# Decay exponents from DRAM rows instead of matmuls, and the rotary additions moved from VectorE to GpSimd

## The chip, the cores and the metric

The kernel runs on one core of a Trainium2 chip. The metric is the device time of one execution in microseconds (us). The kernel before took 1953.01 us, the median of three runs (1952.74 to 1956.06).

## What is computed

A block of a transformer: a routed bias mix, a gated linear attention layer with decay, and the routed bias mix once more, on 2048 tokens of 512 features. Nearly all of the time goes into the attention layer, cut here to what matters (L = 2048, 32 query heads H, 8 key and value heads KVH, head size D = 128, chunks of 128 tokens):

```python
q = (x @ Wq.T).reshape(B, L, H, D);  k, v = ...          # 8 key heads, each repeated for 4 query heads
q, k = q * cos + rot(q) * sin, k * cos + rot(k) * sin    # rot swaps the halves of a head
dt = softplus(x @ Win.T + dt_bias);  g = dt * -exp(A_log_bias)
G = cumsum(g)                                            # inside each chunk, for each head
decay = where(i >= j, exp(G[i] - G[j]), 0)
y_intra = (q @ k.T * decay) @ (v * dt)
state = state * exp(G[-1]) + (k * exp(G[-1] - G)).T @ (v * dt)      # carried from chunk to chunk
y = y_intra + (q * exp(G)) @ state_before
out = (y / rms(y) * gnorm_w * silu(x @ Wg.T)) @ Wo.T
```

## The kernel before

**Tiling.** The outer loop goes over the 8 key heads, called groups g, each with its G = 4 query heads. Inside a group, 16 chunks n of 128 tokens follow each other, since the state is carried. One chunk is one step of every engine. The 4 heads of a group lie side by side in tiles of 128 x 512. Every matmul operand is split into a bf16 high part (suffix H, by ScalarE) and a bf16 low part (suffix L, the remainder), and `mm3` (L286 to L290) issues three matmuls: high by high, high by low, low by high. Matmuls are thus the same three lines everywhere; the operand names tell them apart.

**Fills.** Projections are made one block of 4 chunks (512 tokens) ahead, in ten items: key 0, queries 1 to 4, values 5, gates 6 to 9. `FILLS` puts them in slots A, B and C of the steps: items 0, 1, 2 in step 0 of a block, 3, 4, 5 in step 1, 6, 7 in step 2, and 8, 9 in step 3. Each goes to one of two PSUM banks used in turn (RING, shared with the output projection `project_out`), and a fill waits on `ring_free`, until the bank's last user but one has been read.

**An item's way.** For the key and each query: ScalarE copies the swapped halves (`swap`, QS), VectorE multiplies by the cosines (`rotate` part 0, L1209, which frees the bank), GpSimd multiplies QS by the sines (`times_sin`, L1031), VectorE adds (`rotate` part 1, L1213), ScalarE rounds to bf16 (`hi`, L838 and L840), and the low part is taken: for items 0 and 3 on GpSimd (`lo`, L1036 and L1038), for 1, 2 and 4 on VectorE (`q_lo`, L1217). The turned key is put on B_T by `turn_keys` in step 1 of a block; ScalarE reads it in `keys_hi` (KDH) and VectorE in `keys_lo` (KDL), which frees the bank B_T that the next `turn_z` needs.

**Decay.** GpSimd writes the masked tables MH and ML (`masked_g`, L1049 and L1050) and DM (`masked_dt`, L1054). TensorE multiplies a triangle with MH and ML (L693 and L694), which gives G[i] - G[j] in the bank B_D. ScalarE takes the exponential into PF (L864). VectorE multiplies the scores by DM (L1241) and by PF (L1244). ScalarE and GpSimd split PF into PH and PL (L869, L1077).

**Order.** Every engine runs its own instruction list, written out by hand in its `step`, in order; semaphores link them. The loop over groups is `Fori`; it holds chunks 1 to 15 of one group and chunk 0 of the next. The end of a step on VectorE is `gated` (which waits for GpSimd's RR, L1084), `keys_lo` in step 1 of a block, `add_out`, and then `decayed` of the next step. On ScalarE the end of step 1 is `hi` of item 4 and then `keys_hi`. Weights of the next group are loaded and split in steps 10 to 13 (VectorE L1300, GpSimd L1025), the output weights in step 1 (VectorE L1296). SyncE issues these DMAs, one after the other.

Of the kernel before, what the change touches and what calls it, by code (L numbers as in the profile page):

```python
# [34 lines left out]
EPS = 1e-5  # L35
GW = G * P
# [8 lines left out]
MID = {10: (2,), 11: (5,), 12: (7,), 13: (9,)}  # L45
N_EARLY = sum(len(i) for i in EARLY.values())
# [48 lines left out]
def build(nc, x, cos, sin, masks, wall, rwt, rb, eb2, wint, dtb, alog, gn, out):  # L95
    with ExitStack() as ctx:
# [30 lines left out]
        GH = sb("GH", [P, NCH * H], BF16)  # L127
        GL = sb("GL", [P, NCH * H], BF16)
        IDF = sb("IDF", [P, P])
        MB = sb("MB", [P, 3, P], BF16)  # L130
        DM = sb("DM", [P, G, P])
# [15 lines left out]
        B_S, B_D, B_PV, B_IN, B_CS, B_T = BANK[2:8]  # L147
# [11 lines left out]
        MH = sb("MH", [P, G, P], BF16)  # L159
        ML = sb("ML", [P, G, P], BF16)  # L160
# [18 lines left out]
        with ExitStack() as over:  # L179
# [27 lines left out]
        LTB, TRIB, IDB = MB[:, 0, :], MB[:, 1, :], MB[:, 2, :]  # L207
# [7 lines left out]
        logdecay_full = Sem("logdecay_full", NCH, free=1)  # L215
# [16 lines left out]
        s_ready = Sem("s_ready", NCH, free=1)  # L232
        ql2_ready = Sem("ql2_ready", NB * 3, free=1)
# [8 lines left out]
        ql_ready = Sem("ql_ready", NB * 2, free=2)  # L242
        m_ready = Sem("m_ready", NCH)
        dm_ready = Sem("dm_ready", NCH)
# [22 lines left out]
        d_dot, d_x, d_abs, d_e, d_e2, d_g, d_gh, d_gl, d_cum, d_exp, d_wj = (Sem(n, 1) for n in (  # L267
            "d_dot", "d_x", "d_abs", "d_e", "d_e2", "d_g", "d_gh", "d_gl", "d_cum", "d_exp", "d_wj"))
# [38 lines left out]

        @block.sync
        def _(sp):
# [10 lines left out]
            def load_weights(g):  # L320
                for i in range(NPIECE):

                    if 2 <= i < PO + 2:
                        signal, k = wl_of(i - 2)
                        sp.wait_ge(signal.sem, signal.at(g, k))
                    else:
                        sp.wait_ge(wol_ready.sem, wol_ready.at(g, (i - 2 - PO) if i > PO else i - 2))
                    sp.dma_start(STAGE[:, i % 2, :], wall[g, i] if isinstance(g, int)
                                 else wall[bass.ds(g, 1), i].rearrange("a p n -> (a p) n")).then_inc(w_landed[i % 2].sem, 16)
            load_weights(0)  # L330
            with sp.Fori(1, KVH) as g:
                load_weights(g)
# [290 lines left out]
        def _(pe):  # L623
            for signal in (cs_full, inter_full, intra_full, kt_full, logdecay_full, zt_full):
                pe.sem_inc(signal.sem, signal.free)
# [5 lines left out]
            for k in range(NB):  # L631
# [819 lines left out]
```

## Time and profile before

| | |
|---|---|
| median of three runs | 1953.01 us |
| the profiled execution | 1956.19 us, of which its span is 1954.4 us |
| busy TensorE, matmuls | 1765.2 us (90%) |
| busy VectorE | 1548.2 us (79%) |
| busy GpSimd | 1417.8 us (73%) |
| busy ScalarE | 1032.4 us (53%) |
| mean granted TensorE clock | 0.969 of full speed |
| one group of 16 chunks (809.26 to 1028.90) | 219.64 us |

The profile is taken in one execution and names engines PE (TensorE matmuls), PEld (its weight loads), DVE (VectorE), ACT (ScalarE), POOL (GpSimd). Instructions overlap a little at their ends: a matmul with 512 columns is shown as 379 ns, and the next one starts about 216 ns after it; on POOL and DVE the next instruction starts some 40 and 80 ns before the end shown of the one before. So lengths of a sequence are taken from starts. In a timeline row the bracket gives how long the engine sat idle before, and which instruction ended the wait.

### The profile page before, as it was taken

The page shows a single profiled execution, that of the slowest core. Times are in us where ns is not written, and L with a number is a line of the kernel's source. Part 1 is how long each engine was busy: PE and PEld are TensorE (multiplying, and loading weights), DVE is VectorE, ACT ScalarE, POOL GpSimd, SP SyncE. Part 2 cuts the span into 40 slices and gives each one's busy share as a digit, 9 for nine tenths or more (in the row PEclk, how much of TensorE's full clock was granted, in tenths as well). Part 3 has the DMA queues.
Part 4 walks back from the last instruction along what each step waited for, and adds up shares of the span by engine and source line. Part 5 has one row for each costly group of instructions (what it writes and reads, how often), then busy time and mean ns, then how long its engine had stood idle before and what let it go on. Part 6 is the DMA issues. An engine that isn't in the chain of part 4 may idle for free.

```text
span 1954.4 us, 38786 instructions
## 1 busy us (share of the span) xinstructions
PE 1765.2 (90%) x11904; PEld 997.8 (51%) x11904; DVE 1548.2 (79%) x2955; ACT 1032.4 (53%) x2620; POOL 1417.8 (73%) x1348
## 2 busy tenths in 40 slices
PE   5777998999999998999998998999999998999976
PEld 4544554545455554555454554555455554555544
DVE  6967778787887778787887778787887778787875
ACT  5445555555555555555555555555555555555542
POOL 1348787777777777777777787777777787777743
PEclk9689999999999999999999999999999999999997
DMA  4100001000010001000010001000010001000002
GB/s 162 33 17 23 1 1 49 9 23 2 28 28 24 1 1 49 8 23 2 28 28 24 1 1 49 8 23 2 28 28 24 1 1 46 10 12 1 1 1 86
DMA packets 19515, 43.36 MB, mean 22 GB/s; under 512 B 2656, under 2 KB 3168, under 8 KB 18144
## 3 DMA queue, kind: packets, MB, share of 16 engines
q1 hardware_dynamic: 19296, 40.64, 6.6%
q8 instruction: 113, 1.85, 0.4%
q14 instruction: 106, 0.87, 0.1%
HBM read 36.44 MB, written 4.19 MB: 21 GB/s over the span
## 4 chain that ended last, share of the span: by engine, by line
PE 33%; DVE 22%; issue 18%; POOL 15%; ACT 9%; DVEq 1%; ACTq 0%; POOLq 0%; DMA 0%
PE B L288 10%; PE B L290 9%; PE B L289 9%; DVE YF L1289 2%; POOL QS L1031 2%; POOL WVL L1073 2%; POOL MH L1049 2%; POOL WVF L1065 2%; POOL ML L1050 2%; DVE QF L1209 2%; POOL DM L1054 2%; POOL RR L1084 2%; DVE PF L1244 2%; DVE QF L1213 2%; DVE DM L1241 2%
## 5 line engine op out<-in xcount | busy, mean ns | idle before, releaser
L288 PE MATMUL B<-WH,XTH 128*128 128x512 bf16 (+1 forms) x1024 | 291.6, 306 | 46.6 <-DVE QF L1209 33.5
L1077 POOL TENSOR_TENSOR PL<-PF,PH 128x512 bf16<-128x512 f32 x128 | 155.0, 1211 | 208.3 <-ACT PH L869 208.3
L290 PE MATMUL B<-WH,XTL 128*128 128x512 bf16 (+1 forms) x1024 | 291.2, 305 | 0.0
L289 PE MATMUL B<-WL,XTH 128*128 128x512 bf16 (+1 forms) x1024 | 291.2, 305 | 0.0
L288 PE MATMUL B<-XTH,WH 128*128 128x512 bf16 x640 | 242.7, 379 | 9.8 <-DVE G L1229 7.8
L288 PE MATMUL B<-WH,ZTH 128*128 128x512 bf16 x512 | 194.7, 380 | 53.8 <-DVE QF L1209 33.5
L289 PE MATMUL B<-XTL,WH 128*128 128x512 bf16 x640 | 242.6, 379 | 0.0
L290 PE MATMUL B<-XTH,WL 128*128 128x512 bf16 x640 | 242.6, 379 | 0.0
L869 ACT ACTIVATE PH<-PF 128x512 bf16<-128x512 f32 x128 | 80.8, 631 | 304.6 <-DVE PF L1244 304.6
L1031 POOL TENSOR_TENSOR QS<-QS,SIN 128x512 f32<-128x512 f32 x160 | 228.6, 1429 | 5.2 <-ACT QS L832 5.2
L1305 DVE TENSOR_TENSOR ZTL<-B,ZTH 128x512 bf16<-128x512 f32 x128 | 88.1, 688 | 143.0 <-ACT ZTH L899 143.0
L1049 POOL TENSOR_TENSOR MH<-MB,GH 128x512 bf16<-128x512 bf16 x128 | 133.7, 1045 | 90.3 <-PE B L694 90.2
L290 PE MATMUL B<-WH,ZTL 128*128 128x512 bf16 x512 | 194.0, 379 | 0.0
L289 PE MATMUL B<-WL,ZTH 128*128 128x512 bf16 x512 | 194.0, 379 | 0.0
L892 ACT ACTIVATE SQ<-B 128x128 f32<-128x128 f32 x512 | 134.6, 277 | 80.9 <-DVE B L1256 79.6
L1073 POOL TENSOR_TENSOR WVL<-WVF,WVH 128x512 bf16<-128x512 f32 x120 | 140.2, 1168 | 45.6 <-ACT WVH L876 45.6
L1289 DVE SCALAR_TENSOR_TENSOR YF<-B,RR,G 128x128 f32<-128x128 f32 x512 | 143.6, 342 | 35.0 <-POOL RR L1084 34.9
L288 PEld LDWEIGHTS B<-WH,XTH 128*128 128x128 bf16 x1024 | 103.4, 101 | 128.9 <-DVE QF L1209 39.5
L876 ACT ACTIVATE WVH<-WVF 128x512 bf16<-128x512 f32 x120 | 75.8, 632 | 165.9 <-POOL WVF L1065 165.9
L1084 POOL TENSOR_TENSOR RR<-RM,HALF 128x4 f32<-128x4 f32 x128 | 144.8, 1131 | 19.1 <-POOL RM L1081 16.8
L1278 DVE TENSOR_TENSOR STL<-ST,STH 128x512 bf16<-128x512 f32 x120 | 108.7, 906 | 52.3 <-ACT STH L883 50.2
L1054 POOL TENSOR_TENSOR DM<-MB,DT 128x512 f32<-128x512 bf16 x128 | 143.9, 1124 | 0.0
(164 smaller groups left out, 4984.3 us busy)
## 6 DMA issues: line engine op xcount, KB each, us to landing
STAGE<-in_wall SPq DMA_DIRECT2D x112, 256.0 KB, 2.6
ACC<-in_x SPq DMA_DIRECT2D x4, 1024.0 KB, 7.9
out<-ACC SPq DMA_DIRECT2D x3, 1024.0 KB, 3.9
COS<-in_cos SPq DMA_DIRECT2D x1, 1024.0 KB, 12.9
SIN<-in_sin SPq DMA_DIRECT2D x1, 1024.0 KB, 14.9
out<-ACC SPq DMA_DIRECT2D x4, 256.0 KB, 2.5
EBF<-in_eb SPq DMA_DIRECT2D x1, 256.0 KB, 4.1
MASKS<-in_masks SPq DMA_DIRECT2D x1, 192.0 KB, 4.9
```

Of the source, the lines that this page charges most:

```text
L288: nc.tensor.matmul(out_, ah, bh, start=first, stop=False)
L289: nc.tensor.matmul(out_, ah, bl, start=False, stop=False)
L290: return nc.tensor.matmul(out_, al, bh, start=False, stop=last)
L892: ins = nc.scalar.activation(SQ[:, h, :], B_PV[:, h * P:(h + 1) * P], ACT.Square, scale=float(P) ** -0.5, accum_out=SS[:, h:h + 1])
L1031: nc.gpsimd.tensor_tensor(QS[:, sl, :], QS[:, sl, :], SIN[:, t0:t0 + TB], ALU.mult).then_inc(sin_ready.sem, 1)
L1049: nc.gpsimd.tensor_tensor(MH[:, :, :], tri, tab(GH, g, n)[:, :, None].broadcast_to([P, G, P]), ALU.mult)
L1054: nc.gpsimd.tensor_tensor(DM[:, :, :], TRIB[:, None, :].broadcast_to([P, G, P]), tab(DT, g, n)[:, :, None].broadcast_to([P, G, P]), ALU.mu ...
L1073: nc.gpsimd.tensor_tensor(WVL[:, :], WVF[:, :, :].rearrange("p h e -> p (h e)"), WVH[:, :], ALU.subtract).then_inc(wvl_ready.sem, 1)
L1077: nc.gpsimd.tensor_tensor(PL[:, n % 2, :], PF[:, :], PH[:, n % 2, :], ALU.subtract).then_inc(pl_ready.sem, 1)
L1084: nc.gpsimd.tensor_tensor(RR[:, :], RM[:, :], HALF[:, :], ALU.pow).then_inc(rr_ready.sem, 1)
L1278: nc.vector.tensor_tensor(STL[:, :], ST[:, :], STH[:, :], ALU.subtract).then_inc(stl_ready.sem, 1)
L1289: ins = nc.vector.scalar_tensor_tensor(YF[:, c], B_PV[:, c], RR[:, h:h + 1], G2[:, s + b % 2 * (s == BLK - 1), c], ALU.mult, ALU.mult)
```

## The change

The exponents of the decay no longer come from matmuls. In the preamble the negative cumulative sums (NG) are turned, so that a head's 128 values lie in a row, and are written to DRAM. For every chunk one DMA brings the four heads' rows, broadcast to all 128 partitions, into ROWS (one of two buffers). GpSimd adds a large number where the mask is to be (`mask_rows`), and ScalarE takes exp(-row + NG) in four instructions, one for each head, with the bias by partition. VectorE multiplies scores, dt and decay in four instructions, where it had two of 128 x 512. MH, ML, DM, B_D and their matmuls are gone. Beside this, GpSimd adds the sine part to all five rotated items (`add_sin`) and takes all their low parts (`lo`); VectorE keeps the cosines. GpSimd's and SyncE's steps are written in a new order; ScalarE's and VectorE's keep theirs without the removed instructions.

```diff
+            def load_rows(g, n):
+                at = g + n // NCH
+                if n >= 2:
+                    sp.wait_ge(decay_ready.sem, decay_ready.at(g, n - 2))
+                sp.dma_start(ROWS[:, n % 2, :], (rows_dram[n % NCH, at] if isinstance(at, int)
+                             else rows_dram[n % NCH, bass.ds(at, 1)].rearrange("a n -> (a n)")).partition_broadcast(P)
+                             ).then_inc(rows_landed[n % 2].sem, 16)
...
 def scores(g, n):
-                pe.wait_ge(s_ready.sem, s_ready.at(g, n - 1))
+                pe.wait_ge(p_ready.sem, p_ready.at(g, n - 1))
                 mm3(B_S[:, :], KH[:, par, t:t + P], KL[:, par, t:t + P], QH[:, par, :, t:t + P], QL[:, par, :, t:t + P],
                         True, True).then_inc(scores_full.sem, 1)
-                pe.wait_ge(m_ready.sem, m_ready.at(g, n))
-                pe.wait_ge(decay_ready.sem, decay_ready.at(g, n - 1))
-                nc.tensor.matmul(B_D[:, :], LTB, MH[:, :, :], start=True, stop=False)
-                nc.tensor.matmul(B_D[:, :], LTB, ML[:, :, :], start=False, stop=True).then_inc(logdecay_full.sem, 1)
...
 def decay(g, n):
-                nc.scalar.activation(PF[:, :], B_D[:, :], ACT.Exp).then_inc(decay_ready.sem, 1)
+                for h in range(G):
+                    c = slice(h * P, (h + 1) * P)
+                    ins = nc.scalar.activation(PF[:, c], ROWS[:, n % 2, c], ACT.Exp, bias=tab(NG, g, n)[:, h:h + 1], scale=-1.0)
...
+            def add_sin(g, b, j, use):
+                dst = QF[:, (j - 1) % 2, :] if j else KF[:, :]
+                pool.wait_ge(ring_free.sem, ring_free.at(g, use))
+                pool.wait_ge(sin_ready.sem, sin_ready.at(g, 5 * b + j))
+                nc.gpsimd.tensor_tensor(dst, dst, QS[:, (j + 1) % 2, :], ALU.add).then_inc(qf_ready.sem, 1)
+            def mask_rows(g, n):
+                pool.wait_ge(rows_landed[n % 2].sem, g * (NCH // 2 * 16) + (n // 2 + 1) * 16)
+                rows = ROWS[:, n % 2, :].rearrange("p (h i) -> p h i", h=G)
+                nc.gpsimd.tensor_tensor(rows, rows, AFTER[:, None, :].broadcast_to([P, G, P]), ALU.add).then_inc(rows_masked.sem, 1)
...
 def decayed(g, n):
-                nc.vector.tensor_tensor(dm, B_S[:, :], dm, ALU.mult).then_inc(s_ready.sem, 1)
-                nc.vector.tensor_tensor(PF[:, :], dm, PF[:, :], ALU.mult).then_inc(p_ready.sem, 1)
+                for h in range(G):
+                    c = slice(h * P, (h + 1) * P)
+                    ins = nc.vector.scalar_tensor_tensor(PF[:, c], B_S[:, c], dt[:, h:h + 1], PF[:, c], ALU.mult, ALU.mult)
```

GpSimd, the second half of step 1 of a block, in the kernel before: QS are the sine products of items 3 and 4, RM and RR the norm, then the masked tables of the next step.

```order
L1031 TENSOR_TENSOR QS<-QS,SIN 128x512
L1072 REGISTER_ALU
L1073 TENSOR_TENSOR WVL<-WVF,WVH 128x512
L1054 ISA
L1054 TENSOR_TENSOR DM<-MB,DT 128x512
L1029 REGISTER_ALU
L1031 TENSOR_TENSOR QS<-QS,SIN 128x512
L1081 TENSOR_TENSOR RM<-SS,EPSC 128x4
L1083 REGISTER_ALU
L1084 TENSOR_TENSOR RR<-RM,HALF 128x4
L1049 ISA
L1049 TENSOR_TENSOR MH<-MB,GH 128x512
```

The same place now, from WVL on (the addition to QF is that of item 4, the last query; ROWS is the mask of the next step):

```order
L1113 TENSOR_TENSOR WVL<-WVF,WVH 128x512
L1076 TENSOR_TENSOR QS<-QS,SIN 128x512
L1121 TENSOR_TENSOR RM<-SS,EPSC 128x4
L1123 REGISTER_ALU
L1124 TENSOR_TENSOR RR<-RM,HALF 128x4
L1085 REGISTER_ALU
L1087 TENSOR_TENSOR QL<-QF,QH 128x512
L1080 REGISTER_ALU
L1082 TENSOR_TENSOR QF<-QF,QS 128x512
L1093 REGISTER_ALU
L1095 TENSOR_TENSOR ROWS<-ROWS,AFTER 128x512
```

The addition of item 4 is now GpSimd's, and stands behind the norm and the low part of item 3. VectorE, the end of step 1 before:

```order
L1278 TENSOR_TENSOR STL<-ST,STH 128x512
L1223 TENSOR_TENSOR VL<-B,VH 128x512
L1211 REGISTER_ALU
L1213 TENSOR_TENSOR QF<-QF,QS 128x512
L1289 SCALAR_TENSOR_TENSOR YF<-B,RR,G 128x128 x4
L1234 TENSOR_TENSOR KDL<-B,KDH 128x512
L1309 TENSOR_TENSOR ACC<-ACC,B 128x512
L1241 TENSOR_TENSOR DM<-B,DM 128x512
L1244 TENSOR_TENSOR PF<-DM,PF 128x512
```

And now, up to the low part of the turned key (the addition to QF is gone from between VL and YF):

```order
L1244 REGISTER_ALU
L1249 TENSOR_TENSOR QF<-B,COS 128x512
L1309 TENSOR_TENSOR STL<-ST,STH 128x512
L1254 TENSOR_TENSOR VL<-B,VH 128x512
L1320 SCALAR_TENSOR_TENSOR YF<-B,RR,G 128x128 x4
L1265 TENSOR_TENSOR KDL<-B,KDH 128x512
```

## Rows read from the trace of the kernel before

**Rows 1.** The page: busy time of the engines, busy tenths of PE in 40 slices.

```profile
PE 1765.2 (90%) x11904; PEld 997.8 (51%) x11904; DVE 1548.2 (79%) x2955; ACT 1032.4 (53%) x2620; POOL 1417.8 (73%) x1348
...
PE   5777998999999998999998998999999998999976
```

**Rows 2.** Windows: the four blocks of one group; us, PE, PEld, DVE, ACT, POOL, clock.

```profile
809.26:865.13 55.87, 52.15 (x342) 29.19 (x341) 43.97 (x78) 30.63 (x78) 41.85 (x40) 0.97 0.07 21
865.13:918.13 53.00, 51.52 (x353) 28.30 (x352) 41.26 (x80) 28.04 (x75) 42.21 (x40) 1.00 0.01 1
918.13:973.70 55.57, 51.87 (x353) 28.15 (x352) 45.75 (x83) 29.89 (x79) 43.93 (x40) 1.00 0.08 25
973.70:1028.90 55.20, 50.88 (x350) 27.95 (x349) 45.52 (x78) 30.66 (x79) 43.02 (x42) 1.00 0.09 25
```

**Rows 3.** Timeline of PE in the second block: start, duration, instruction, idle before.

```profile
865.13 0.38 PE L288 MATMUL B<-QH,KH 128*128 128x512 bf16 x1
...
865.77 0.38 PE L693 MATMUL B<-MH,MB 128*128 128x512 bf16 x1
...
866.21 0.38 PE L288 MATMUL B<-XTH,WH 128*128 128x512 bf16 x1
...
899.21 0.61 PE L735 MATMUL B<-IDF,YF 128*128 128x128 f32 x4
...
907.92 0.39 PE L288 MATMUL B<-WH,XTH 128*128 128x512 bf16 x1 [0.53 <-DVE G L1229]
```

**Rows 4.** Instructions of a tile on POOL: shortest, median and longest duration in ns.

```profile
L1031 POOL TENSOR_TENSOR QS<-QS,SIN x160: 1261/1271/1811, 118.7 to 1823.8; 128x512 f32<-128x512 f32 x160
L1077 POOL TENSOR_TENSOR PL<-PF,PH x128: 1152/1158/1600, 148.0 to 1872.6; 128x512 bf16<-128x512 f32 x128
L1065 POOL TENSOR_TENSOR WVF<-VF,WJ x120: 1033/1042/1492, 150.1 to 1864.4; 128x512 f32<-128x512 f32 x120
L1049 POOL TENSOR_TENSOR MH<-MB,GH x128: 1032/1041/1486, 135.3 to 1860.0; 128x512 bf16<-128x512 bf16 x128
L1081 POOL TENSOR_TENSOR RM<-SS,EPSC x128: 192/203/667, 163.0 to 1881.4; 128x4 f32<-128x4 f32 x128
L1084 POOL TENSOR_TENSOR RR<-RM,HALF x128: 1007/1008/1552, 163.3 to 1881.6; 128x4 f32<-128x4 f32 x128
```

**Rows 5.** Timeline of ACT in the second block, swap of item 1 and end of step 1.

```profile
874.02 0.59 ACT L831 ACTIVATE QS<-B 64x512 f32<-64x512 f32 x1 [1.04 <-PE B L290]
...
895.13 0.63 ACT L838 ACTIVATE QH<-QF 128x512 bf16<-128x512 f32 x1 [1.35 <-DVE QF L1213]
895.67 0.58 ACT L858 ACTIVATE KDH<-B 128x512 bf16<-128x512 f32 x1
```

**Rows 6.** Timeline of DVE in the second block, from the last addition on.

```profile
894.42 0.68 DVE L1213 TENSOR_TENSOR QF<-QF,QS 128x512 f32<-128x512 f32 x1
...
897.04 0.68 DVE L1234 TENSOR_TENSOR KDL<-B,KDH 128x512 bf16<-128x512 f32 x1
...
898.24 0.69 DVE L1241 TENSOR_TENSOR DM<-B,DM 128x512 f32<-128x512 f32 x1
898.96 0.69 DVE L1244 TENSOR_TENSOR PF<-DM,PF 128x512 f32<-128x512 f32 x1
...
902.01 0.68 DVE L1229 SCALAR_TENSOR_TENSOR G<-TH,B 128x512 f32<-128x512 f32 x1
...
904.02 1.11 DVE L1270 SCALAR_TENSOR_TENSOR ST<-ST,DCH,B 128x128 f32<-128x128 f32 x4
...
907.19 0.67 DVE L1229 SCALAR_TENSOR_TENSOR G<-TH,B 128x512 f32<-128x512 f32 x1
```

**Rows 7.** Timeline rows around the loop's turn and the weights.

```profile
967.10 2.68 DVE L1300 TENSOR_TENSOR WL<-STAGE,WH 128x512 bf16<-128x512 f32 x2 [1.30 <-ACT WH L816]
...
1046.75 0.60 ACT L864 ACTIVATE PF<-B 128x512 f32<-128x512 f32 x1 [2.93 <-issue]
```

**Rows 8.** The page: DMA issues, KB each, us to landing.

```profile
STAGE<-in_wall SPq DMA_DIRECT2D x112, 256.0 KB, 2.6
```

More of the change, by code:

```diff
@@ new lines, in _, with step @@
+            for f in range(NB):
+                sp.wait_ge(d_rows.sem, d_rows.at(f, 0))
+                sp.dma_start(rows_dram[f * BLK:(f + 1) * BLK].rearrange("c g (h t) -> (c g h) t", h=G), NGT[:, f, :]).then_inc(d_sent.sem, 16)
+                if f == 0:
+                    sp.wait_ge(d_sent.sem, 16)
+                    for n in range(2):
+                        load_rows(0, n)
+            sp.wait_ge(d_sent.sem, 16 * NB)
+            load_rows(0, 2)
+            load_rows(0, 3)
+            def step(g, n, last):
+                if not (last and n >= NCH - 3):
+                    load_rows(g, n + 3)
+                if n == 1:
+                    for i in range(PO + 2, NPIECE):
+                        load_piece(g, i)
+                if not last:
+                    for i in LOADS.get(n, ()):
+                        load_piece(g + 1, i)
@@ L334, in _ @@
+            with sp.Fori(0, KVH - 1) as g:
+                for n in steps(False):
+                    step(g, n, False)
+            for n in steps(True):
+                step(KVH - 1, n, True)
             for k in range(NB - 1):
@@ L1109, in _, with step @@
-            masked_dt(0, 0)
-            masked_g(0, 1)
+            pool.wait_ge(after_ready.sem, 1)
+            mask_rows(0, 0)
+            mask_rows(0, 1)
             p_lo(0, 0)
-            masked_dt(0, 1)
             weighted_v(0, 0)
             wv_lo(0, 0)
-            def step(g, n, last):
+            def step(g, n, last, first=False):
                 b, s = divmod(n, BLK)
-                def sine(x):
-                    if filled(n, last).get(x, PV_) < PV_:
-                        times_sin(g, b + 1, filled(n, last)[x])
+                ring = ring_order(last)
+                now = {x: i for x, i in filled(n, last).items() if i < PV_}
+                before = {x: i for x, i in filled(n - 1, last).items() if i < PV_} if n else {}
@@ L1122, in step, with add @@
                 nxt = not (last and n == NCH - 1)
+                def add(x):
+                    if x in now:
+                        add_sin(g, b + 1, now[x], now[x] - FIRST if first else ring[("F", b, now[x])])
                 if not (last and n >= NCH - 2):
-                    masked_g(g, n + 2)
+                    mask_rows(g, n + 2)
+                if "C" in before:
+                    add_sin(g, (n - 1) // BLK + 1, before["C"], -1 if n == 1 else ring[("F", (n - 1) // BLK, before["C"])])
@@ L1132, in step @@
                 if not filled(n, last):
                     inv_rms(g, n)
[L1134 removed]
+                add("A")
+                if nxt:
                     wv_lo(g, n + 1)
[L1136 to L1140 removed]
+                if "B" in now:
+                    times_sin(g, b + 1, now["B"])
                 if filled(n, last):
```

211 lines of the change are left out of this document (89 added, 122 removed).

## The prediction, made before the changed kernel was run

> **What bounds the kernel now.** I read the page first. TensorE is busy 90% of the span, and nine tenths or more in nearly every slice from the fifth to the last but two; VectorE has 79%, GpSimd 73% [rows 1]. So a matmul that goes should count, unless something else has little slack. The windows by block say how little: the four blocks of a group take 55.87, 53.00, 55.57 and 55.20 us, and GpSimd is busy 42 to 44 us of each [rows 2]. Then the timeline of PE in the second block, the one without weights and without the loop's turn. Its matmuls of 512 columns start 0.216 us apart (three score matmuls take from 865.13 to 865.77) and the pair on MH and ML takes 865.77 to 866.21, 0.43 us [rows 3]. The turn of the gated output in step 2 (L735) starts at 899.21, 34.08 us after the block's start, and the block ends at 918.13, 18.92 later [rows 2, 3]. Between, PE waits once more, 0.53 us (0.70 by starts) for a gate on VectorE [rows 3]. TensorE is the bound, but in every block it meets VectorE's order two or three times.
>
> **What is removed on PE.** 128 pairs of 0.43 us, 55 us in all. This is the most that the change can give, and 1953 less 55 is 1898.
>
> **What moves to GpSimd.** Removed in each step: MH, ML and DM, at about 1.04 us a piece (MH's row; a spacing of 1.00), 12 us a block. Added in each step: the mask on ROWS. No row shows it. It reads two full f32 tiles as the sine product does (1.27) and broadcasts as WVF does (1.04) [rows 4]; I take 1.23, the spacing of the first, which it is nearest to, and keep 1.00. Added in each block: five additions of the sine's form (1.23) and three low parts of PL's form (1.12) [rows 4]: 9.5 us. With the masks, 14.4 us come for 12.0 that go. The sum of GpSimd grows by 2.4 us a block, still under TensorE's. But the masks went from all four steps, and the additions come into the first two.
>
> **The path in steps 0 and 1.** Count from the block's start, T. Fill B of step 0 (item 1) now ends 0.43 earlier than before, so its swap starts at 874.02 less 865.13 less 0.43, or 8.46, takes two halves of 0.6 [rows 5], and GpSimd can begin the sine product at 9.7. From there it has, without a gap that I can find (each input is ready before its turn): sine of item 1, RM and RR, low 0, add 1, sine 2; next step: mask, add 2, PL, low 1, WVF, low 2, sine 3, add 3, WVL, sine 4, RM and RR, low 3, add 4. These are nine of 1.23, six of 1.12, one of 1.00 and two norm pairs (0.20, a gap, 1.01: 1.33 together) [rows 4]: 11.1 + 6.7 + 1.0 + 2.7 = 21.5. Add 4 ends at 31.2 without any lengthening. Durations on GpSimd have a second value 0.44 to 0.54 above the first [rows 4]; I count it once for each STL, the instruction of VectorE left in each step that reads two SBUF tiles while GpSimd is busy: 0.9. So 32.1.
>
> Who waits for add 4? ScalarE, in order: `hi` of item 4, and behind it `keys_hi`, whose input is long there. Before, `hi` waited 1.35 us for VectorE's addition, which started at 894.42, 29.3 after T [rows 5, 6]. From the addition's end it takes `hi` 0.54, KDH 0.58, KDL 0.68 and three handovers, 1.95 us, until B_T is free [rows 5, 6]: 34.05. The turn in step 2 of PE needs B_T. Without waits it would arrive at about 31.2: 34.08 less three pairs of 0.43, less the 1.6 that are left when the matmuls before it are counted at their spacing of 0.216 (a quarter of it for 128 columns, 0.44 for four turns). So it waits some 2.8 us in all, and starts at 34.05: where it started before. **All of PE's gain in steps 0 to 2 is spent there.**
>
> Behind KDL on VectorE stand the output's addition and `decayed`, and for them wait PH, the gate's tanh, ZTH, ZTL and the gate G (902.01). From KDL's end (897.72) to G's (902.69) it took 4.97 [rows 6]. `decayed` was 1.41 (898.24 to 899.65) and is four of ST's form, 1.11 [rows 6], so 4.67. PE needs G 4.35 after its turn (0.44 + 1.32 + 2.59), and waits 0.3. From G to the next G there were 5.18 us [rows 6]; here collisions can take off some 0.3, PE wants it after 3.24 of matmuls, and waits 1.2 to 1.6 where it waited 0.70. The 18.92 held one pair and this wait: 18.92 - 0.43 - 0.70 + 0.3 + 1.3 = 19.4. **Second block: 34.05 + 19.4 = 53.4, against 53.00: 0.4 longer.**
>
> **The other blocks.** Third block, steps 2 and 3: two weight splits on VectorE in each step (2.6 us [rows 7]) make VectorE's loop longer than PE's work. It starts 1.46 later (34.05 against KDL's end at 32.59) and gives back 0.3 a step by the shorter `decayed`: +0.8. Fourth block: GpSimd's split in step 12 is put ahead of the sine of item 2 (1.12), two splits on VectorE lengthen GpSimd by 0.45 each, and the block starts with the wait that the third hands on. Turn at 37.5, and 19.4 less 0.65 (the last chunk updates no state): 56.3 against 55.20, +1.1. First block: the loop's turn costs ScalarE 2.93 us [rows 7] inside the GpSimd path, since `hi` of item 1 now ends late and the exponentials and PH stand behind it: GpSimd waits some 1.2 for PH, and output weights on VectorE lengthen it by 1.4 to 1.8. Turn at 37.5, block 56.9 against 55.87: +1.0.
>
> **Costs put at nothing.** The rows' DMA: a transfer of 256 KB lands in 2.6 us [rows 8], is issued when a buffer is free, at the start of a step, and is used a step later; SyncE queues it behind weight loads only in steps 1 and 10 to 13, where it still has half a step. If a broadcast took three times 2.6 it would be as well. The four exponentials (at most 1.2 against 0.6) stand where ScalarE waited. The preamble adds four turns and four DMAs, and GpSimd's additions there replace VectorE's; it loses four casts: between -3 and +3, taken as 0.
>
> **Sum.** Eight groups of (1.0 + 0.4 + 0.8) and seven fourth blocks of 1.1 (the last group fills nothing there): 17.6 + 7.7 = 25.3. The last four chunks are a loop over VectorE and lose 0.3 each: -1.2. Total +24 us. Against the profiled execution (span 1954.4, 1956.19 in all) that is 1980; the median of the runs lies 3.2 below, so **1977 us, 1.2% slower**.
>
> A rule on the collisions: by the Trainium skill (GPSIMD Engine Reference, Specifications) GpSimd's SBUF interfaces are shared with VectorE and contend with instructions of VectorE that have two SBUF inputs. That speaks for the change here, as the additions leave VectorE; the two values in [rows 4] agree. By this rule two collisions are left in the path, which is what I count; if they cost nothing, the sum would be 0.9 x 31 = 28 us lower, at about 1949.
>
> **Rivals.**
> (A) *GpSimd's path is shorter, and TensorE stays the bound.* For it: the sum of GpSimd grows only by 2.4 us a block, and the mask may cost 1.00. Against it: the list above has no gap, and the path would have to be 3 us shorter in 22. Then steps 0 to 2 save three pairs and steps with gates little: 1.3 us a block, 31 blocks, 40 us: 1913. Half of it, 1935, if the path is 1.5 shorter.
> (B) *Both cancel.* Path at 31.2 + 0.5, so that a block is 0.8 shorter than I say: -0.4 to 0 against before: 1950 to 1957.
> (C) *The longer waits also cost clock.* The first window's clock is 0.97 against 1.00 in the others [rows 2], a loss of 0.03 x 55.87 or 1.7 us at the lower of two levels, after waits of that block. Waits of 3 to 6 us in two blocks of a group could add 16 such stretches, 27 us: 2004. Against it: they would fall where PE waits for gates anyway.
> (D) *Rows come late:* the mask waits for the DMA, in every step by the time beyond the half step. It decides only from a landing of about 8 us on, three times the row; then 1 us a step, 128 steps, 2105. I give it little.
>
> **Chances.** Forecast (1962 to 1995) 0.52; A 0.22; B 0.11; C 0.12; D 0.03. By 0.2% (about what a measurement of this kernel tells from no change): faster 0.25, same 0.10, slower 0.65. The forecast alone reaches 1962 to 1995; the range for 8 in 10 takes in B, half of A, and C: 1930 to 2004.
>
> **What would show it.** In the changed profile: GpSimd without a wait from the sine of item 1 to the addition of item 4, over some 22 us; KDH right behind `hi`, with ScalarE's wait ending on a GpSimd addition at L1082; PE's longest waits before the turn (L735's successor) in step 2 of every block, some 2 to 3 us, ended by VectorE's KDL; GpSimd busy about 1500 us, TensorE's matmul sum less by its 256 instructions, and a mean of PE under 90%. A second block of 53.4, a fourth of 56.3. The prediction is wrong if that wait is under 1 us, or ends on ZTL or a gate instead, if the mask takes under 1.0, or if GpSimd stands idle between those two instructions.

## The result

The changed kernel takes 2014.7 us, the median of four runs (2013.5 to 2020.67); the kernel before, timed beside it, took 1954.53. The ratio is 1.0306, with a 95% interval of 1.0271 to 1.0341: **3.1% slower**. The prediction said slower and gave 1977 with a range that ended at 2004. The direction was right, the size was not: 60 us, not 24. Of the executions of the experiments below one stands apart: one of e11_mask2 took 3567 us, which no profile shows; its interval leaves it out, and without it the median is 2040.6.

### The profile page after: what moved, and what is told of

It reads as the page before. It is cut to its first block, busy times and chain, and to the rows that moved or that the text cites. A ratio compares the mean times of both kernels' runs of the same rounds, so it can differ in the third digit from the quotient of the medians.

```text
span 2018.9 us, 39366 instructions
## 1 busy us (share of the span) xinstructions
PE 1740.0 (86%) x11652; PEld 972.2 (48%) x11652; DVE 1269.7 (63%) x2956; ACT 1117.0 (55%) x3012; POOL 1427.6 (71%) x1340
## 4 chain that ended last, share of the span: by engine, by line
POOL 44%; issue 26%; PE 11%; DVE 10%; ACT 6%; POOLq 1%; DVEq 0%; ACTq 0%; DMA 0%; SPq 0%
POOL QS L1076 10%; POOL QF L1082 7%; POOL QL L1087 6%; POOL WVL L1113 5%; POOL RR L1124 3%; POOL ROWS L1095 3%; POOL WVF L1105 3%; PE B L287 3%; PE B L288 3%; PE B L289 3%; POOL KF L1082 2%; ACT SQ L934 2%; POOL WL L1070 2%; POOL RM L1121 1%; DVE PF L1274 1%
## 5 line engine op out<-in xcount | busy, mean ns | idle before, releaser
L1117 POOL TENSOR_TENSOR PL<-PF,PH 128x512 bf16<-128x512 f32 x128 | 150.9, 1179 | 276.9 <-ACT PH L911 276.5
L1076 POOL TENSOR_TENSOR QS<-QS,SIN 128x512 f32<-128x512 f32 x160 | 210.5, 1315 | 12.3 <-ACT QS L871 11.8
L877 ACT ACTIVATE QH<-QF 128x512 bf16<-128x512 f32 x128 | 80.3, 627 | 228.1 <-POOL QF L1082 228.1
L1113 POOL TENSOR_TENSOR WVL<-WVF,WVH 128x512 bf16<-128x512 f32 x120 | 151.3, 1261 | 45.4 <-ACT WVH L918 45.4
L1274 DVE SCALAR_TENSOR_TENSOR PF<-B,DT,PF 128x128 f32<-128x128 f32 x512 | 143.8, 343 | 46.8 <-ACT PF L905 45.4
L905 ACT ACTIVATE PF<-ROWS,NG 128x128 f32<-128x128 f32 x512 | 162.8, 397 | 13.9 <-POOL ROWS L1095 13.9
L1082 POOL TENSOR_TENSOR QF<-QF,QS 128x512 f32<-128x512 f32 x128 | 162.8, 1272 | 4.4
L1095 POOL TENSOR_TENSOR ROWS<-ROWS,AFTER 128x512 f32<-128x512 f32 x128 | 162.7, 1271 | 0.0
```

Of the source, the lines that this page charges most:

```text
L905: ins = nc.scalar.activation(PF[:, c], ROWS[:, n % 2, c], ACT.Exp, bias=tab(NG, g, n)[:, h:h + 1], scale=-1.0)
L1076: nc.gpsimd.tensor_tensor(QS[:, sl, :], QS[:, sl, :], SIN[:, t0:t0 + TB], ALU.mult).then_inc(sin_ready.sem, 1)
L1082: nc.gpsimd.tensor_tensor(dst, dst, QS[:, (j + 1) % 2, :], ALU.add).then_inc(qf_ready.sem, 1)
L1095: nc.gpsimd.tensor_tensor(rows, rows, AFTER[:, None, :].broadcast_to([P, G, P]), ALU.add).then_inc(rows_masked.sem, 1)
L1113: nc.gpsimd.tensor_tensor(WVL[:, :], WVF[:, :, :].rearrange("p h e -> p (h e)"), WVH[:, :], ALU.subtract).then_inc(wvl_ready.sem, 1)
L1117: nc.gpsimd.tensor_tensor(PL[:, n % 2, :], PF[:, :], PH[:, n % 2, :], ALU.subtract).then_inc(pl_ready.sem, 1)
```

## The profile after

The page's busy times and PE's busy tenths, which answer to [rows 1]. The span is 2018.9 us (the execution took 2020.67, 5 above the next of the four).

```profile
PE 1740.0 (86%) x11652; PEld 972.2 (48%) x11652; DVE 1269.7 (63%) x2956; ACT 1117.0 (55%) x3012; POOL 1427.6 (71%) x1340
...
PE   5667998889988998889988998889989998889976
```

PE has lost its 256 matmuls, 25 us of busy time, VectorE 279 us, and GpSimd has gained only 10, where the prediction had 77 ("busy about 1500 us"). The instructions that GpSimd has in both kernels became shorter in the mean: the 160 sine products (QS) 1.32 us for 1.43, the 32 low parts of the key (KL) 1.16 for 1.59. No engine is at its limit, and the span grew by 64.5. The time is in waits. The four blocks of a group, as windows with the columns of [rows 2]:

```profile
845.64:903.53 57.89, 50.01 (x333) 26.61 (x332) 35.63 (x79) 32.98 (x91) 43.95 (x41) 1.00 0.12 38
903.53:957.31 53.78, 50.01 (x346) 27.53 (x345) 32.83 (x80) 30.65 (x88) 41.87 (x40) 1.00 0.07 21
957.31:1013.89 56.58, 51.84 (x345) 28.41 (x344) 37.10 (x82) 31.91 (x89) 42.60 (x39) 0.97 0.15 43
1013.89:1074.30 60.41, 51.88 (x342) 28.06 (x341) 36.02 (x78) 34.13 (x94) 44.70 (x42) 0.94 0.14 40
```

Three blocks grew by 2.0, 0.8 and 1.0 us against [rows 2]; the fourth grew by 5.2. Where the starts of the score matmuls divide both spans, the account is this:

| part of the span | before | after | measured | predicted |
|---|---|---|---|---|
| up to step 0 | 146.5 | 158.8 | +12.3 | 0 |
| eight first blocks | 451.7 | 461.6 | +9.9 | +8.0 |
| eight second blocks | 423.4 | 429.7 | +6.3 | +3.2 |
| eight third blocks | 441.4 | 449.2 | +7.8 | +6.4 |
| seven fourth blocks | 386.4 | 423.0 | +36.6 | +7.7 |
| last steps | 17.9 | 15.4 | -2.6 | -1.2 |
| what follows them | 87.1 | 81.2 | -6.0 | 0 |

**The predicted path, in the second block (T is 903.53).** PE's timeline: the scores begin the block with no MH behind them, and its waits are ahead of the output's turn (L772, in the kernel before L735), ahead of the output projection and ahead of a gate.

```profile
903.96 0.38 PE L289 MATMUL B<-QH,KL 128*128 128x512 bf16 x1
904.18 0.38 PE L287 MATMUL B<-XTH,WH 128*128 128x512 bf16 x1
...
937.76 0.65 PE L772 MATMUL B<-IDF,YF 128*128 128x128 f32 x4 [2.07 <-DVE KDL L1265]
...
942.58 0.39 PE L287 MATMUL B<-WH,ZTH 128*128 128x512 bf16 x1 [0.26 <-DVE G L1260]
...
947.10 0.39 PE L287 MATMUL B<-WH,XTH 128*128 128x512 bf16 x1 [1.11 <-DVE G L1260]
```

The turn comes at T+34.23 (predicted 34.05, after a wait of 2.8; it was 2.07) and the rest takes 19.55 (predicted 19.4). The two waits that end with VectorE's G are 1.37 in all (predicted 1.6). In [rows 3] the only one was 0.53. GpSimd's timeline from the block's start to the addition of item 4:

```profile
907.31 1.16 POOL L1117 TENSOR_TENSOR PL<-PF,PH 128x512 bf16<-128x512 f32 x1 [2.62 <-ACT PH L911]
...
913.26 1.27 POOL L1076 TENSOR_TENSOR QS<-QS,SIN 128x512 f32<-128x512 f32 x1
...
916.96 1.27 POOL L1082 TENSOR_TENSOR QF<-QF,QS 128x512 f32<-128x512 f32 x1
918.18 1.28 POOL L1076 TENSOR_TENSOR QS<-QS,SIN 128x512 f32<-128x512 f32 x1
919.41 1.28 POOL L1095 TENSOR_TENSOR ROWS<-ROWS,AFTER 128x512 f32<-128x512 f32 x1
920.64 1.29 POOL L1082 TENSOR_TENSOR QF<-QF,QS 128x512 f32<-128x512 f32 x1
922.23 1.16 POOL L1117 TENSOR_TENSOR PL<-PF,PH 128x512 bf16<-128x512 f32 x1 [0.30 <-ACT PH L911]
...
929.23 1.61 POOL L1113 TENSOR_TENSOR WVL<-WVF,WVH 128x512 bf16<-128x512 f32 x1
...
934.49 1.26 POOL L1082 TENSOR_TENSOR QF<-QF,QS 128x512 f32<-128x512 f32 x1
```

The sine of item 1 starts at T+9.73 and the addition of item 4 ends at T+32.2; 9.7 and 32.1 were predicted. Beside the short gaps between RM and RR, which the prediction had, there is one, 0.30 us, where PL waits for PH. It looks like nothing, and it matters below. The reader can check a collision here: WVL is 1.61 us against 1.15 elsewhere while VectorE runs STL, which starts at 929.10. By the Trainium skill (GPSIMD Engine Reference, Specifications) the two engines contend when VectorE reads two SBUF inputs; the trace agrees with that, as [rows 4] did.

ScalarE and then VectorE at the end of step 1, where [rows 5] and [rows 6] had the same instructions:

```profile
935.79 0.63 ACT L877 ACTIVATE QH<-QF 128x512 bf16<-128x512 f32 x1 [4.88 <-POOL QF L1082]
936.32 0.58 ACT L897 ACTIVATE KDH<-B 128x512 bf16<-128x512 f32 x1
936.80 1.26 ACT L905 ACTIVATE PF<-ROWS,NG 128x128 f32<-128x128 f32 x4
```

```profile
936.93 0.69 DVE L1265 TENSOR_TENSOR KDL<-B,KDH 128x512 bf16<-128x512 f32 x1 [2.37 <-ACT KDH L897]
937.54 0.68 DVE L1340 TENSOR_TENSOR ACC<-ACC,B 128x512 f32<-128x512 f32 x1
938.28 1.13 DVE L1274 SCALAR_TENSOR_TENSOR PF<-B,DT,PF 128x128 f32<-128x128 f32 x4
```

ScalarE waits 4.88 us where it waited 1.35 in [rows 5], and two things stand behind that rounding in its queue which do not need it: KDH and the four exponentials. The four take 1.26 us together (0.39 each, overlapping), where one of 0.60 stood [rows 7]. By the Trainium skill (ScalarE: Activation LUTs, What ACT_TABLE_LOAD costs) a bias by partition is an operand with a price of its own, and the estimate from its figures is 387 ns for 128 columns; the trace agrees (392 ns median).

**What the prediction missed, in the fourth block.** PE, and GpSimd before it:

```profile
1051.15 0.61 PE L287 MATMUL B<-WH,XTH 128*128 128x512 bf16 x1 [3.99 <-POOL WL L1070]
1051.55 0.63 PE L288 MATMUL B<-WL,XTH 128*128 128x512 bf16 x1
```

```profile
1047.61 1.16 POOL L1087 TENSOR_TENSOR QL<-QF,QH 128x512 bf16<-128x512 f32 x1
1048.72 1.26 POOL L1082 TENSOR_TENSOR QF<-QF,QS 128x512 f32<-128x512 f32 x1
1049.94 1.15 POOL L1070 TENSOR_TENSOR WL<-STAGE,WH 128x512 bf16<-128x512 f32 x1
1051.05 1.27 POOL L1095 TENSOR_TENSOR ROWS<-ROWS,AFTER 128x512 f32<-128x512 f32 x1
```

The low part of weight piece 9 (MID[13], L1070) stands behind the addition of item 4. PE's next fill needs this weight, waits 3.99 us, and resumes at the lower of the clock's two levels: the next matmul starts 0.40 us later where it took 0.22, and the window's clock is 0.94. In the list of PE's waits (what waits, for whom, us in total, times, the longest) it stands fourth, behind the turn:

```profile
PE B L772 <- DVE KDL L1265: 39.5, 24, 2.1
PE B L287 <- POOL WL L1070: 27.9, 7, 4.0
```

In the kernel before the same low part stood near the end of GpSimd's step 13 as well, but with fewer instructions ahead of it, and the first fill of step 14 started 0.31 us after its end:

```profile
1006.60 1.16 POOL L1025 TENSOR_TENSOR WL<-STAGE,WH 128x512 bf16<-128x512 f32 x1
```

```profile
1008.07 0.38 PE L288 MATMUL B<-WH,XTH 128*128 128x512 bf16 x1
```

**The first block** (T is 845.64). Here PL of step 1 waits 2.61 us for PH, where the prediction had some 1.2:

```profile
867.16 1.51 POOL L1117 TENSOR_TENSOR PL<-PF,PH 128x512 bf16<-128x512 f32 x1 [2.61 <-ACT PH L911]
```

```profile
884.07 0.65 PE L772 MATMUL B<-IDF,YF 128*128 128x128 f32 x4 [0.90 <-DVE KDL L1265]
```

The turn starts at T+38.43 (predicted 37.5) and the rest takes 19.46, so the 1.0 us by which this block is longer than predicted lies ahead of the turn.

**The rows' DMA** costs nothing in the loop. It lands in 3.1 us beside the 2.6 of [rows 8], and GpSimd never waits for one in the loop:

```profile
ROWS<-rows_dram SPq DMA_DIRECT2D x128, 256.0 KB, 3.1
```

**The preamble.** ScalarE waits for the turned rows ahead of the weights' high parts, and the weight DMA released by these is late in turn (the kernel before reached the same place at 101.24, after a wait of 4.14 us):

```profile
105.10 0.28 ACT L654 ACTIVATE NGT<-B 128x128 f32<-128x128 f32 x1 [2.54 <-PE B L650]
105.27 1.14 ACT L855 ACTIVATE WH<-STAGE 128x512 bf16<-128x512 f32 x2
109.71 0.63 ACT L855 ACTIVATE WH<-STAGE 128x512 bf16<-128x512 f32 x1 [3.30 <-DMA STAGE<-in_wall]
```

## The experiments

All are timed in four or five runs, against seven or eight of the kernel before on the same chip (1950.8 to 1951.0 us). Ratios are to these, that of the changed kernel to its own 1954.53; so where two kernels are close, the ratios compare them and not the times. Blocks are those of one group in the middle of the trace.

| kernel | us | ratio, interval | blocks |
|---|---|---|---|
| changed | 2014.7 | 1.0306 [1.0271, 1.0341] | 57.9 53.8 56.6 60.4 |
| e1_gate9 | 1994.2 | 1.0222 [1.0194, 1.025] | 57.9 53.8 56.6 57.3 |
| e2_keys | 1981.8 | 1.0151 [1.0123, 1.0178] | 57.4 53.7 56.1 56.8 |
| e8_exps | 1911.1 | 0.9787 [0.9761, 0.9813] | 54.0 50.8 53.6 56.2 |
| e12_exps_only | 1993.8 | 1.0223 [1.0205, 1.0241] | 56.6 53.3 56.1 59.4 |
| e10_lows | 1959.2 | 1.0041 [1.0027, 1.0056] | 57.3 51.9 54.8 56.4 |
| e5_nomask | 2010.6 | 1.0304 [1.0272, 1.0335] | 58.1 53.8 56.6 59.3 |
| e11_mask2 | 2042.1 | 1.0467 [1.0446, 1.0488] | 57.9 54.8 57.6 61.5 |
| e3_dram_only | 1923.2 | 0.9847 [0.982, 0.9874] | 56.4 50.9 53.7 54.2 |
| e4_move_only | 2144.7 | 1.0997 [1.0958, 1.1037] | 61.1 59.0 61.5 61.6 |
| e6_pre | 2011.3 | 1.0299 [1.0271, 1.0326] | 57.9 53.8 56.6 60.4 |
| e9_best | 1887.4 | 0.9654 [0.9624, 0.9684] | 54.9 50.3 52.8 53.7 |
| e13_split | 1872.4 | 0.9604 [0.9588, 0.962] | 54.9 50.3 51.5 53.1 |

In e5_nomask and e11_mask2 the fourth blocks are not alike: they take 58.3 to 59.8 and 59.0 to 61.5 us, group by group.

### The weight behind the addition (e1_gate9)

```diff
-EARLY = {10: (0, 1), 11: (3, 4), 12: (6,), 13: (8,)}
-MID = {10: (2,), 11: (5,), 12: (7,), 13: (9,)}
+EARLY = {10: (0, 1), 11: (3, 4), 12: (6,), 13: (8, 9)}
+MID = {10: (2,), 11: (5,), 12: (7,)}
```

> The changed kernel, with the low part of weight piece 9 (the gates' last) taken by VectorE at the start of step 13 instead of GpSimd behind the addition of item 4. Theory 1 (GpSimd's instruction list sets the time: in steps 0 and 1 of a block the turn waits for the addition of item 4, and in the fourth block step 14's first gate fill waits 4 us for this low part): the fourth block falls from 60.4 to 56 to 57.5 us, the others keep 57.9, 53.8 and 56.6; seven groups save about 4 us each, 1983 to 1990 us in all. Rival, theory 2 (the decay part costs: the rows' DMA, the four exponentials, the four products): the fourth block's 5 us are not in this wait, and the time stays within 10 us of 2014.7.

Measured: 1994.2, 4 above the expected range. The wait is gone, and the fourth block as a window:

```profile
1000.56:1057.85 57.29, 50.52 (x337) 28.77 (x341) 36.72 (x79) 33.95 (x94) 44.01 (x41) 0.97 0.14 42
```

60.4 has become 57.3 and the other blocks are unchanged to 0.03. Seven fourth blocks give 22 us in the traces, the ratios 16. The missed wait is shown. It is not all of what was missed: of the 5.2 us, 3.1 went; 2.1 stayed, where 1.1 was predicted. The turn of this block comes at T+39.07 (43.27 in the changed kernel, 37.5 predicted), and TensorE does not wait for KDL ahead of it, as the prediction had it, but earlier, 2.84 us for VectorE's cosine product.

### The two parts apart (e3_dram_only, e4_move_only)

The first has the rows, the mask and the split exponentials, with VectorE's additions and low parts and GpSimd's order as before. The second keeps the decay matmuls, MH, ML and DM, and has the additions and low parts on GpSimd, in the changed order.

```diff
 e3: GpSimd's step of before, with
-masked_g(g, n + 2)
-masked_dt(g, n + 2)
+mask_rows(g, n + 2)
...
 e4: GpSimd's step of after, with
-mask_rows(g, n + 2)
+masked_g(g, n + 2)
...
+masked_dt(g, n + 2)
```

> Only the first half of the change: exponents from DRAM rows, mask on GpSimd, four exponentials and four products; VectorE adds the sine parts and takes the low parts of items 1, 2 and 4 as in the kernel before, and GpSimd's order is the old one. Theory 1: TensorE is the bound again, less 0.43 us a step, with VectorE's waits kept; a block without weights falls from 53.0 to 51 to 52, the turn's wait for KDL is gone; 1910 to 1935 us, faster than before. Theory 2: not faster than before, 1955 us or more.

> Only the second half of the change: the kernel before with its matmuls on MH and ML and its masked tables, but GpSimd adds the sine parts and takes all low parts, in the changed kernel's order (the table DM stands before the second sine product). Theory 1: GpSimd's path from the sine of item 1 to the addition of item 4 holds two masked tables in place of one mask and a DM, so it is about 1.8 to 2.8 us longer than in the changed kernel, and blocks are as much longer: 2070 to 2110 us. Theory 2: near the kernel before, under 1990 us.

Measured: 1923 and 2145. The rows alone are 1.5% faster than before, inside the expected range; the move to GpSimd turns that into 3.1% slower, 90 us on top of the rows and 194 us without them. The expectation for the second was too low by 35. There GpSimd is busy 50 to 53 us of each block of 59 to 62, so that it comes near to being the bound by its sum as well.

### The mask, left out and doubled (e5_nomask, e11_mask2)

e5_nomask leaves the mask on later tokens out (and takes the bias from another table of the same size). e11_mask2 adds it twice.

```diff
 e5
-                    mask_rows(g, n + 2)
...
 e11
+                nc.gpsimd.tensor_tensor(rows, rows, AFTER[:, None, :].broadcast_to([P, G, P]), ALU.add).then_inc(rows_once.sem, 1)
+                pool.wait_ge(rows_once.sem, rows_once.at(g, n))
```

> The changed kernel without GpSimd's mask on ROWS (128 instructions of 1.27 us); ScalarE waits for the rows' DMA itself, and takes exp with another finite bias, so the decays computed are not those wanted. Theory 1: one mask stands in GpSimd's path from sine 1 to addition 4, so each block whose turn waits for KDL is 1.0 to 1.3 us shorter (53.8 becomes 52.6), and the time is 1972 to 1985 us. Theory 2: the mask is in steps where GpSimd has time, and the rows still come by DMA: 2005 to 2015 us.

The theory of the prediction, that the mask of step 1 lies in the path, failed here: 2010.6, and the second block stayed at 53.8. GpSimd's timeline of it shows why:

```profile
910.94 1.27 POOL L1082 TENSOR_TENSOR QF<-QF,QS 128x512 f32<-128x512 f32 x1
913.57 1.16 POOL L1117 TENSOR_TENSOR PL<-PF,PH 128x512 bf16<-128x512 f32 x1 [1.36 <-ACT PH L911]
```

GpSimd ends the addition of item 2 1.06 us earlier (T+17.34 for T+18.40) and waits 1.06 longer for PH (1.36 for 0.30), so PL starts at the same point, T+18.7. The path goes another way round: the addition of item 1, its rounding, the exponentials behind that, VectorE's product, PH, PL; in the changed kernel this and GpSimd's own list end within 0.30 us of each other. If that is so, removing work of GpSimd there gives nothing and adding it costs all but 0.30:

> The changed kernel with the mask added twice (1.24 us more of GpSimd in every step; the value behind the exponential is 0 either way). Without the mask the blocks kept their length to 0.03 us. Theory 1 (the mask lies in GpSimd's wait for PH, which is 0.30 us in step 1 of the second block and over 2 us in the others): the second block grows by 1.24 less 0.30, to 54.7, the other blocks alike, some 25 to 30 us more: 2038 to 2048. Rival (the mask is hidden as a whole, as its removal suggests): 2010 to 2018.

Measured: the second block takes 54.75, where 54.7 was expected, and PL there starts without a wait:

```profile
924.08 1.15 POOL L1120 TENSOR_TENSOR PL<-PF,PH 128x512 bf16<-128x512 f32 x1
```

The whole takes 2042 us. The third block grew by 1.0 as well, but not the first, which kept its 57.9: its PL had 2.61 us of waiting to give. The reader should keep this pair: an instruction whose removal gives nothing was 0.30 us from costing its full length.

### What stands in GpSimd's row behind PL (e10_lows)

```diff
 GpSimd's step
-                if "B" in before:
-                    lo(g, (n - 1) // BLK + 1, before["B"])
...
-                if "C" in before:
-                    lo(g, (n - 1) // BLK + 1, before["C"])
...
 VectorE's step, behind decayed(g, n + 1)
+                    if (n - 1) % BLK == 0:
+                        q_lo(g, (n - 1) // BLK + 1, before["B"])
+                        q_lo(g, (n - 1) // BLK + 1, before["C"])
```

> The changed kernel with the low parts of items 1, 2 and 4 back on VectorE; the additions stay on GpSimd. Theory 1 (GpSimd's row of instructions from PL to the addition of item 4 sets the end of step 1): two low parts of 1.12 us leave it, the addition of item 4 ends at T+30.0 instead of T+32.2 in the second block, which takes 51.5 to 52.0 where it took 53.8; with the other blocks 45 to 60 us less than the changed kernel: 1955 to 1970. Rival (the additions themselves cost, by VectorE's cosine product that waits for the low part of the key, 63 us in 31 waits): little changes, 2000 to 2012.

Measured: 1959.2, second block 51.9. Three low parts of 1.12 us a block, two of which stand between PL and the addition of item 4, are worth 2.6% of the time: in that stretch the path does go through GpSimd.

### What is queued on ScalarE (e2_keys, e12_exps_only, e8_exps)

Three orders of the end of ScalarE's step. e2_keys and e8_exps also have the weight pieces of e1_gate9.

```diff
                 slot("C", 0)
-                slot("B", 1)
                 if s == 1 and filled(n, last):
                     keys_hi(g, b + 1)
+                if not (last and n + 2 > NCH - 1):      # e8, e12
+                    decay(g, n + 2)                     # e8, e12
+                slot("B", 1)
...
                 if nxt:
-                    decay(g, n + 1)                     # e8, e12
```

> The kernel of e1_gate9 with one line moved: ScalarE reads the turned key (keys_hi, KDH) before it rounds item 4 (hi), instead of behind it. In e1_gate9 TensorE waits 2.07 us for KDL before the output's turn in the second and the third block of a group and 0.9 in the first (39.5 us in 24 waits). Theory 1 (what binds is the chain addition of item 4, hi, the exponentials, VectorE's decayed, and the wait at the turn is only where TensorE meets it): hi now ends 0.0 us later and only KDH (0.48 us between starts) leaves the chain in front of the exponentials, so a second block is 0.5 us shorter (53.3), the wait for KDL vanishes and the one for the gate G or for the output product grows by 1.5; 31 blocks by 0.5 are 15 us: 1975 to 1985. Rival (the wait for KDL is itself the loss, and what follows it is TensorE's own work): second block 51.7, 40 us less: 1950 to 1958.

Measured: 1981.8, 12 us less than e1_gate9. TensorE's waits (us in total, times, the longest) in e1_gate9, and then the one for gates in e2_keys:

```profile
PE B L287 <- DVE G L1260: 54.9, 57, 2.5
PE B L772 <- DVE KDL L1265: 42.1, 27, 2.1
```

```profile
PE B L287 <- DVE G L1260: 81.6, 52, 4.3
```

The wait for KDL is gone (it is 42.1 us in e1_gate9; the 39.5 of the expectation is the changed kernel's); what TensorE waits for gates grew by 27. The second block takes 53.3 us in four of the groups and 53.7 in three, those with a stretch at the clock's lower level (0.97). A wait of 2 us in front of the turn was worth 0.1 to 0.5 us: it was a place where TensorE met the chain, not its cause.

> The changed kernel with only the exponentials ahead of the rounding of items 1 and 4 on ScalarE; keys_hi stays behind it and the weights stay as they are. Theory 1 (VectorE reaches decayed only behind KDL, and KDL waits for keys_hi, which waits for the addition of item 4): decayed comes 0.1 to 0.2 us earlier, the second block 53.3 to 53.6 instead of 53.8: 1998 to 2010. Rival (the 71 us that e8_exps gained on e2_keys belong to the exponentials alone): 1940 to 1960.

Measured: 1993.8, a little under the expected range; second block 53.3. The exponentials alone are not it either.

> The kernel of e2_keys with the exponentials of the next chunk also ahead of the rounding (hi) of items 1 and 4 on ScalarE, at the end of a step. Nothing is taken from GpSimd: its list of additions, low parts and masks is the same. Theory 1 (GpSimd's addition counts only because ScalarE's keys_hi and exponentials are queued behind the rounding that waits for it): VectorE's decayed starts right behind the output's addition, at about T+32.4 in the second block where it started at T+34.8, PH follows, and TensorE is the bound again but for short waits: second block 51.0 to 51.8, and 31 blocks by 2 to 2.7 less: 1915 to 1940. Rival (GpSimd's list is the bound by its sum, 13.5 us from PL to the addition of item 4 and behind it the mask, PL and WVF): the second block stays at 53 or above, time 1970 to 1985.

Measured: **1911.1, 2.1% faster than before**, with every addition, low part and mask still on GpSimd; it is busy 1422 us. GpSimd, ScalarE and PE at the end of step 1 (T is 853.09):

```profile
883.70 1.26 POOL L1084 TENSOR_TENSOR QF<-QF,QS 128x512 f32<-128x512 f32 x1
```

```profile
880.00 0.60 ACT L897 ACTIVATE KDH<-B 128x512 bf16<-128x512 f32 x1
880.48 1.28 ACT L905 ACTIVATE PF<-ROWS,NG 128x128 f32<-128x128 f32 x4
884.99 0.63 ACT L877 ACTIVATE QH<-QF 128x512 bf16<-128x512 f32 x1 [3.23 <-POOL QF L1084]
```

```profile
884.99 0.61 PE L772 MATMUL B<-IDF,YF 128*128 128x128 f32 x4
```

The addition of item 4 ends at T+31.9, only 0.35 us earlier than in the changed kernel (the gap of 0.30 is gone, as PH comes earlier too). But now only its own rounding waits for it. The turn starts at T+31.9 without a wait, 2.3 us earlier, and the second block takes 50.8. Removing KDH alone from behind the rounding gave 12 us, removing the exponentials alone 16 to 21, both 83 (against e1_gate9; 104 with the weight): as long as one of them is behind it, VectorE's `decayed` is.

### The preamble (e6_pre)

```diff
                 if k >= 2:
                     act_sums(act, k - 2)
-                    act_rows(act, k - 2)
...
                 act_turned2(act, k)
+                if k >= 2:
+                    act_rows(act, k - 2)
```

> The changed kernel with only its preamble altered: ScalarE's copy of the turned rows (act_rows) stands behind act_turned2 instead of ahead of the weights' high parts, so that no weight waits for it. In the changed kernel ScalarE waits 2.5 to 3.0 us for the turn there, then 3.3 us for a weight DMA that was released late, and the first rotated item starts 4.9 us later than before where the rest of the preamble is alike. Theory 1: the first swap starts 3.5 to 5 us earlier and the whole is that much shorter, 2010 to 2012. Rival (the wait is covered by the normalisation of the tokens that follows): no change, 2013 to 2016.

Measured: 2011.3, with a ratio that overlaps the changed kernel's, so the times do not tell. In the traces the first swap starts at 113.8 us (116.7 in e9_best and 112.9 in e13_split, with the same edit), against 117.7 to 122.7 in the nine profiles of kernels with the preamble of the change, and 114.1 before. So the wait for the turn is a part of the delay, some 5 us of it; e4_move_only, which turns no rows, has its first swap at 114.0. Of the changed kernel's 12.3, 3.7 belong to its one profiled execution (its normalisation starts at 113.62, that of e1_gate9, with the same instructions, at 109.87).

### Better than both (e9_best, e13_split)

e9_best is e3_dram_only with the edits of e6_pre and e8_exps (not the weight piece). e13_split adds:

```diff
-EARLY = {10: (0, 1), 11: (3, 4), 12: (6,), 13: (8,)}
-MID = {10: (2,), 11: (5,), 12: (7,), 13: (9,)}
+EARLY = {10: (0,), 11: (3,), 12: (6,), 13: (8,)}
+MID = {10: (1, 2), 11: (4, 5), 12: (7,), 13: (9,)}
```

> The rows from DRAM with VectorE's additions and three low parts (as e3_dram_only), the preamble of e6_pre, and on ScalarE keys_hi and the exponentials ahead of the rounding of items 1 and 4 (as e8_exps). e3_dram_only took 1923 us with a second block of 50.85, in which TensorE still waits 0.77 and 0.77 us for VectorE's cosine product, and the four exponentials stand before decayed. Theory 1: a step that ends with a rounding gives 0.5 to 1.0 us, blocks 50.85 to about 50.3, first block 56.3 to about 55.5, preamble 4 less: 1895 to 1912. Rival (the cosine product behind VectorE's full list binds there, and ScalarE's order does not matter): only the preamble's 4 us, 1917 to 1921.

> The kernel of e9_best with one weight piece in step 10 and one in step 11 split by GpSimd instead of VectorE, which has two there. Theory 1 (the third block is 2.5 us longer than the second because VectorE has two splits of 1.3 us in a step, while GpSimd waits 363 us for PH): third block 52.8 to about 51.5, seven times: 1875 to 1882. Rival (GpSimd's two splits in a row delay the weighted values or the mask): third block 53 or more, 1887 to 1895.

Measured: 1887.4 and 1872.4, a little below both ranges. The page of e13_split, busy times:

```profile
PE 1696.6 (91%) x11652; PEld 968.1 (52%) x11652; DVE 1455.1 (78%) x3198; ACT 1116.8 (60%) x3012; POOL 1183.4 (63%) x1098
```

The best kernel is 4.0% faster than before, and TensorE is its bound again at 91%. The rows are worth having; the move to GpSimd is not, even with ScalarE's order mended (e8_exps, 1911, against e9_best, 1887). The two differ in the preamble and in one weight piece too. By their traces the difference is 15.7 us, of which 14 are in the fourth blocks, where VectorE and GpSimd also split weights.

## Why the prediction was right in direction and wrong in size

**The step that failed is the fourth block's term**, "Turn at 37.5 ... 56.3 against 55.20, +1.1". It counted GpSimd's split of step 12 as something that lengthens the path to the turn, and did not ask who waits for the split of step 13, which the changed order leaves behind the addition of item 4. Measured +5.2 in each of seven blocks, 36.6 us against 7.7; e1_gate9 takes 22 of the 29 missing back. The trace of before could have shown it: the same split started at 1006.60, 32.9 us after the block's start, 0.4 before step 14, whose fill reads it. It had 0.31 us of slack; in the changed kernel it starts 36.1 after. The path that the term did count is not the one that was left when the wait was gone: the turn was to wait for KDL and come at 37.5, and comes at 39.07 without that wait (e1_gate9).

**The preamble's term** was sized 0 (between -3 and +3) and measured +12.3, of which 3.7 is this execution's. "The preamble adds four turns" counted their work, 0.3 us each, not that ScalarE waits for two of them in front of the weights, 2.69 and 2.54 us. GpSimd's additions there make each item 3.57 us of one engine in series, and the last rounding comes 21.95 us after the first swap where it came 19.4 after; that is 2.5 us, and e4_move_only, with these additions and without turned rows, has the same (22.0). But e3_dram_only, with the additions on VectorE, has 22.7, so something in the rows' part lengthens it too; what, is open.

**The second and third blocks** came out at +0.8 and +1.0 for +0.4 and +0.8, and the second by the stations predicted, to 0.2 us at each. A part of that is luck: of the 0.9 us counted for two collisions one came, 0.46, and the gap of 0.30 for PH and a smaller one ahead of the addition of item 3 filled the rest. **The first block** came out at +2.0 for +1.0: PL waited 2.61 us for PH there, not 1.2. The end of the run was 6.0 us shorter for 0; that stays open, and e9_best and e13_split, alike in that part, differ by 4.5 there.

**"From there it has, without a gap that I can find"** was right about the end and wrong about the path; by the prediction's own sign (GpSimd idle between those two instructions) it failed, by 0.30 us. The mask of step 1 is not on it (e5_nomask); the exponentials are, and the prediction cost them at nothing because "ScalarE waited" there. A wait of ScalarE in front of them says only that they begin late. They lay behind an instruction that the change delays.

**Of the rivals,** A (GpSimd's path is shorter) fell: the path ended at T+32.2. B fell with it. C (clock) came as forecast in the clock and not in the time: the third block's clock is 0.97 and the fourth's 0.94, where [rows 2] had 1.00 for both. But the third blocks of e1_gate9 take 56.6 us at 0.97 and the same at 1.00, and its fourth blocks 57.3 at either; the lower level cost nothing in these blocks, which wait anyway. In the fourth blocks of e8_exps, which wait less, it goes with 1.5 us (54.7 at 1.00, 56.2 at 0.97). What it cost in the changed kernel's fourth block, behind the missed wait, is not separated from that wait. D (late rows) fell: 3.1 us, no wait.

**"This is the most that the change can give", 55 us for the matmuls:** the rows alone gave 30 in e3_dram_only, and with ScalarE's order mended and two weight pieces moved 78 in e13_split, more than the 55. That `decayed`, MH, ML and DM, and waits went too may explain it; ScalarE's order and the two weight pieces were not tried on the kernel before, so how much of the 78 they would give without the rows is not shown.

## What to carry to other kernels

When work moves to another engine, ask what is queued *behind the instruction that waits for it*, on every engine on the way: here the same additions and low parts on GpSimd cost 90 us (against e3_dram_only) or some 24 (e8_exps against e9_best), by whether KDH and the exponentials, which do not need the rounding, stood behind it on ScalarE. Then list every consumer of each instruction that a new order pushes back, those without a wait today above all, and take how near to its use each one lands. And an experiment that takes work away and finds nothing has not shown slack; do the opposite one too.

## What was not expected of the hardware

Four exponentials of 128 x 128 from SBUF with a bias by partition take 1.26 us, one of 128 x 512 from PSUM 0.60. The broadcast of a row to 128 partitions, 256 KB, landed in 3.1 us beside 2.6 for a plain load of that size, 128 times, with DMA engines busy 7 to 15% of a block.
